# A macaron block on one core: query rows in two kinds, one scratch write per batch, four groups of position products per tile

## The reference

```
content = einsum('bhsp,bhtp->bhst', q + u, k)
pos     = relative_shift(einsum('bhsp,htp->bhst', q + v, sinusoid @ Wp + bp))
weights = softmax((content + pos) / sqrt(8));  out = (weights @ val) @ Wo + bo
```

## Time and profile before

| | us |
|---|---|
| median of the runs | 445.53 |
| the profiled execution: its time | 447.46 |
| its span, first to last instruction | 445.3 |
| VectorE busy | 398.2 (89%) |
| TensorE busy (matmuls) | 357.0 (80%) |
| ScalarE busy | 263.9 (59%) |
| GpSimd busy | 113.4 (25%) |

### The profile page before, as it was taken

The page is one execution under the profiler, slowest core; times in us unless marked ns, Lnnn a source line. Parts: engine busy times, 40 slices in busy tenths (PEclk is TensorE's granted clock), DMA queues, the critical chain, the costliest instruction groups (busy, mean ns, idle before and its releaser), DMA issues.

```text
span 445.3 us, 18049 instructions
## 1 busy us (share of the span) xinstructions
PE 357.0 (80%) x7328; PEld 288.1 (65%) x7328; DVE 398.2 (89%) x579; ACT 263.9 (59%) x650; POOL 113.4 (25%) x157
## 2 busy tenths in 40 slices
PE   1869898756979889898898987988989889676974
PEld 1647675645767767677676766776767767573664
DVE  8786988429999999999999999999999999948685
ACT  1666555316666666666666666666666666614980
POOL 7543745390020201202102022020120210025552
PEclk9988899969899999999999999999999999988898
DMA  7005147920322313213133132231321301500002
GB/s 213 1 1 186 51 148 245 296 62 12 81 57 43 81 26 87 68 31 84 40 65 75 19 88 56 44 80 20 88 64 30 89 7 25 75 18 2 0 26 71
DMA packets 60182, 30.67 MB, mean 69 GB/s; under 512 B 36880, under 2 KB 58928, under 8 KB 60016
## 3 DMA queue, kind: packets, MB, share of 16 engines
q1 hardware_dynamic: 59376, 29.22, 25.8%
q10 hardware_dynamic: 576, 0.73, 0.6%
q0 software_dynamic: 192, 0.18, 0.2%
HBM read 19.11 MB, written 11.01 MB: 68 GB/s over the span
## 4 chain that ended last, share of the span: by engine, by line
DVE 58%; issue 17%; PE 11%; ACT 5%; POOL 2%; SPq 2%; DMA 2%; DVEq 1%; POOLq 0%; ACTq 0%
DVE pT L894 30%; DVE negmax L886 19%; PE pair L1014 3%; ACT v_rep L602 2%; DVE xh L702 2%; ACT v_rep L590 1%; PE pair L969 1%; DVE v_rep L820 1%; DVE sqsum L814 1%; DMA qs_scratch<-pT 1%; SPq L309 1%; PE pair L1183 1%; DMA stage_k<-kc_scratch 1%; DVE stat L692 1%; PE pair L1116 1%
## 5 line engine op out<-in xcount | busy, mean ns | idle before, releaser
L633 ACT ACTIVATE probs<-pair,negmax 128x512 f32<-128x512 f32 x256 | 173.7, 683 | 111.3 <-DVE negmax L886 111.3
L886 DVE TENSOR_REDUCE negmax<-pair 128x2 f32<-128x1024 f32 x128 | 152.1, 1188 | 10.4 <-PE pair L1133 10.4
L894 DVE STREAM_TRANSPOSE pT<-probs 128x1024 f32<-128x1024 f32 x128 | 157.0, 1226 | 0.5 <-ACT probs L633 0.5
L1116 PE MATMUL pair<-stage_k,stage_c 128*32 128x512 f16 x1024 | 117.2, 408 | 47.4 <-ACT probs L633 40.8
L1122 PE MATMUL pair<-stage_z,stage_q 128*32 128x512 f16 x1024 | 111.4, 384 | 0.0
L1133 PE MATMUL pair<-stage_z,stage_q 128*32 128x438 f16 (+58 forms) x1024 | 102.9, 282 | 0.0
L508 POOL COPY v_diag<-v_rep 32x512 f32 (+1 forms) x64 | 38.9, 607 | 233.9 <-PE pair L1148 226.5
L1128 PE MATMUL pair<-stage_z,stage_q 128*32 128x16 f16 (+50 forms) x1024 | 97.9, 277 | 0.0
L1148 PE MATMUL pair<-pT,v_diag 128*32 128x128 f32 (+1 forms) x2176 | 93.3, 271 | 3.6 <-DVE pT L894 3.6
L1116 PEld LDWEIGHTS pair<-stage_k,stage_c 128*32 128x32 f16 x1024 | 50.7, 140 | 69.5 <-ACT probs L633 55.4
L1148 PEld LDWEIGHTS pair<-pT,v_diag 128*32 128x32 f32 x2176 | 73.3, 114 | 4.1 <-DVE pT L894 3.8
(11 more groups left out here) (112 smaller groups left out, 326.0 us busy)
## 6 DMA issues: line engine op xcount, KB each, us to landing
stage_z<-z_scratch SPq DMA_DIRECT2D x16, 254.0 KB
qs_scratch<-pT SPq DMA_DIRECT2D x12, 256.0 KB, 2.7
stage_q<-qs_scratch SPq DMA_DIRECT2D x126, 24.0 KB
stage_z<-z_scratch SPq DMA_DIRECT2D x16, 128.0 KB
qc_scratch<-pT SPq DMA_DIRECT2D x8, 256.0 KB, 3.5
kc_scratch<-pT SPq DMA_DIRECT2D x8, 256.0 KB, 3.5
stage_k<-kc_scratch SPq DMA_DIRECT2D x16, 128.0 KB
stage_z<-z_scratch SPq DMA_DIRECT2D x16, 127.5 KB
```

The lines of the kernel that those rows point to most:

```text
L633: nc.scalar.activation(probs[:, q % 6, :], score_pair(q // 2)[:, q % 2, :], ACT.Exp, bias=negmax[:, q % 8:q % 8 + 1], accum_out=rowsum[:, ...
L886: nc.vector.tensor_reduce(negmax[:, 2 * n % 8:2 * n % 8 + 2], score_pair(n)[:, :, :], AX.X, ALU.max, negate=True).then_inc(max_ready, 1)
L894: nc.vector.transpose(pT[:, par, 2 * n:2 * n + 2, :].rearrange("p a s -> p (a s)"), probs[:, 2 * n % 6:2 * n % 6 + 2, :].rearrange("p a s ...
L1116: mm(bank[32 * j:32 * j + 32, :], all_rows[:, 32 * j:32 * j + 32], stage_k[:, par, :], start=True, stop=False, skip_group_check=True)
```

## The change

The query scratch keeps, per batch and head element, the row of vl and the row of vh (576 columns each), written by one DMA. stage_q holds for each block of 64 query rows the rows themselves and the rows one group further on, side by side, and each row pair carries low and high halves. Positions come in two sets, high (low = 0) and low (low = 1), each a part of 512 columns and a part of ZR = 510 columns. So each tile has four groups of position products instead of three: for each set the left part and the right part. The low x low product, which was left out, is now part of the sum. The scratch of content queries and keys is laid out by head and batch. SP waits for GpSimd's copies before its first write of a batch, and writes in the order queries, content, keys.

```
-    qs_dram = nc.dram_tensor("qs_scratch", (D, 2, 3, B * S), F16, kind="Internal").ap()
-    qc_dram = nc.dram_tensor("qc_scratch", (D, 4, B * S), F16, kind="Internal").ap()
-    kc_dram = nc.dram_tensor("kc_scratch", (D, 4, B, S), F16, kind="Internal").ap()
-    z_dram = nc.dram_tensor("z_scratch", (D, 2, 3, 2 * S), F16, kind="Internal").ap()
+    qs_dram = nc.dram_tensor("qs_scratch", (D, 2, B, VW), F16, kind="Internal").ap()
+    qc_dram = nc.dram_tensor("qc_scratch", (H, B, 2, HP, 2, S), F16, kind="Internal").ap()
+    kc_dram = nc.dram_tensor("kc_scratch", (H, B, 2, HP, 2, S), F16, kind="Internal").ap()
+    z_dram = nc.dram_tensor("z_scratch", (D, 2, 4, 2 * S), F16, kind="Internal").ap()
...
-        stage_q = sb("stage_q", [128, 2, 3, B * S], F16)
+        stage_q = sb("stage_q", [128, 2, B * NI, 2, NG], F16)
-        stage_z = sb("stage_z", [128, 2, 3, ZW], F16)
+        stage_z = sb("stage_z", [128, 2, 2, S + ZR], F16)
...
         def stage_queries(eng, h, par, done, rows_i=range(NI)):
-            q_rows = qs_dram.rearrange("(h p) t k n -> h (p t) k n", p=HP)[h]
+            q_rows = qs_dram.rearrange("(h p) t b n -> h (p t) b n", p=HP)[h]
             for ii in rows_i:
                 i = NI - 1 - ii
-                src = q_rows.rearrange("r k (b m) -> r (k b) m", b=B)[:, :, i * NG:(i + 1) * NG]
-                dst = stage_q[16 * ii:16 * ii + 16, par, :, :].rearrange(
-                    "r k (b m) -> r (k b) m", b=B)[:, :, i * NG:(i + 1) * NG]
-                eng.dma_start(dst, src).then_inc(done, 16)
+                dst = stage_q[16 * ii:16 * ii + 16, par, :, :, :].rearrange("r (b i) k g -> r b i (k g)", b=B)[:, :, i]
+                eng.dma_start(dst, q_rows[:, :, i * NG:(i + 2) * NG]).then_inc(done, 16)
+
+        def write_queries(eng, b, r, done):
+
+            eng.dma_start(qs_dram[r, :, b, :], rep_ap(vl[r, b, :], [(VQ, 2), (1, VW)])).then_inc(done, 16)
+
+        def write_content(eng, b, h0, h1, done):
+            c = slice(b * S, (b + 1) * S)
+            for a in range(2):
+                eng.dma_start(qc_dram[h0:h1, b, a].rearrange("h p d n -> h (p d n)"), half[HP * h0:HP * h1, 0:2, c])\
+                    .then_inc(done, 16)
+
+        def write_keys(eng, b):
+            c = slice(b * S, (b + 1) * S)
+            for a in range(2):
+                eng.dma_start(kc_dram[:, b, a].rearrange("h p d n -> h (p d n)"),
+                              rep_ap(half[:, 2 + a, c], [(0, 2), (1, S)])).then_inc(k_out, 16)
...
-            for t, kind, src in ((0, 0, 0), (1, 0, 2), (0, 1, 0), (1, 1, 1), (0, 2, 2), (1, 2, 3)):
-                sp.dma_start(z_dram[:, t, kind, :], zs[:, src, :]).then_inc(z_out, 16)
+            for t in range(2):
+                sp.dma_start(z_dram[:, t, :, :], zs).then_inc(z_out, 16)
...
-                for kind, lo, hi in ((0, 0, ZW), (1, 0, S), (2, ZB0, ZW)):
-                    zr = z_rows[:, kind, :]
-                    src = bass.AP(zr.tensor, zr.offset + lo, [[1, NI]] + [list(zr.ap[0])] + [[1, hi - lo]])
-                    sp.dma_start(stage_z[:, par, kind, lo:hi], src).then_inc(staged[par], 16)
+                for low in range(2):
+                    for kind, lo, at, n in ((low, 0, 0, S), (2 + low, ZB0, S, ZR)):
+                        zr = z_rows[:, kind, :]
+                        src = bass.AP(zr.tensor, zr.offset + lo, [[1, NI]] + [list(zr.ap[0])] + [[1, n]])
+                        sp.dma_start(stage_z[:, par, low, at:at + n], src).then_inc(staged[par], 16)
...
-                sp.wait_ge(q_split, 2 * b + 1)
-                sp.dma_start(qs_dram[:, :, 1, c], rep_ap(vh[:, b, :], [(0, 2), (1, S)])).then_inc(q_out, 16)
                 sp.wait_ge(v_extended, 2 * b + 2)
-                sp.dma_start(qs_dram[:, :, 0, c], rep_ap(vl[:, b, :], [(NG, 2), (1, S)])).then_inc(q_out, 16)
-                sp.dma_start(qs_dram[:, :, 2, c], rep_ap(vh[:, b, NG:], [(0, 2), (1, S)])).then_inc(q_out, 16)
-
+                write_queries(sp, b, slice(0, D), q_out)
                 sp.wait_ge(q_split, 2 * b + 2)
...
-            for par, n in ((0, 0), (0, 1), (0, 2), (1, 0), (1, 1)):
-                nc.vector.memset(stage_q[:, par, n, :].bitcast(U32), 0).then_inc(stage_zero, 1)
+            for par in range(2):
+                for b in (0, 2):
+                    nc.vector.memset(stage_q[:, par, b * NI:(b + 2) * NI, :, :].bitcast(U32), 0)\
+                        .then_inc(stage_zero, 1)
...
-            nc.gpsimd.memset(stage_q[:, 1, 2, :].bitcast(U32), 0).then_inc(stage_zero, 1)
...
+                for low in range(2):
+                    for j in range(4):
+                        a0 = 128 * j + NI * q
+                        n = a0 + NI
+                        m0 = S - NI - a0
+                        mm(bank[32 * j:32 * j + 32, 0:n], stage_q[:, par, :, 0, j * NQ + q],
+                           stage_z[:, par, low, m0:m0 + n], start=False, stop=False, skip_group_check=True)
+                    for j in range(4):
+                        a0 = 128 * j + NI * q
+                        n = S - a0 - 2
+                        ins = mm(bank[32 * j:32 * j + 32, a0 + 2:S], stage_q[:, par, :, 1, j * NQ + q],
+                                 stage_z[:, par, low, S:S + n], start=False, stop=low == 1, skip_group_check=True)
```

More of the change, by code:

```diff
@@ L53 @@
 LOADS_FIRST = 6
[L54 removed]
+LOADS = 17
+ZR = ZW - ZB0
 def macaron_kernel(nc, ins, out):
     x_d, w12_d, vectors_d, rows_d, wqkv_d, wo_d, wp_emb_d, ident_d = ins
[L61 to L64 removed]
+    qs_dram = nc.dram_tensor("qs_scratch", (D, 2, B, VW), F16, kind="Internal").ap()
+    qc_dram = nc.dram_tensor("qc_scratch", (H, B, 2, HP, 2, S), F16, kind="Internal").ap()
+    kc_dram = nc.dram_tensor("kc_scratch", (H, B, 2, HP, 2, S), F16, kind="Internal").ap()
+    z_dram = nc.dram_tensor("z_scratch", (D, 2, 4, 2 * S), F16, kind="Internal").ap()
     at_dram = nc.dram_tensor("attn_scratch", (H, HP, 16, 128), F32, kind="Internal").ap()
@@ L119, in macaron_kernel @@
         uh, ul, kh, kl = (half[:, n, :] for n in range(4))
+        VQ = 2 * (14336 - 8192)
         vl = pTf[:, 8192:8192 + B * VW // 2].bitcast(F16).rearrange("p (b n) -> p b n", b=B)
@@ L291, in stage_content @@
         def stage_content(eng, h, par, b, done):
-            c_rows = qc_dram.rearrange("(h p) t n -> h (p t) n", p=HP)[h]
+            rows32 = qc_dram.rearrange("h b a p d n -> h b (a p d) n")[h][b]
             dst = stage_c[32 * b:32 * b + 32, par, :].rearrange("r (j b m) -> r j b m", j=4, b=B)[:, :, b]
-            src = c_rows[:, b * S:(b + 1) * S].rearrange("r (j m) -> r j m", j=4)
-            eng.dma_start(dst, src).then_inc(done, 16)
+            eng.dma_start(dst, rows32.rearrange("r (j m) -> r j m", j=4)).then_inc(done, 16)
@@ L298, in stage_keys @@
         def stage_keys(eng, h, par, done):
-            k_rows = kc_dram.rearrange("(h p) t b n -> h b (p t) n", p=HP)[h]
-            eng.dma_start(stage_k[:, par, :], k_rows).then_inc(done, 16)
+            eng.dma_start(stage_k[:, par, :], kc_dram.rearrange("h b a p d n -> h (b a p d) n")[h]).then_inc(done, 16)
         def stage_queries(eng, h, par, done, rows_i=range(NI)):
-            q_rows = qs_dram.rearrange("(h p) t k n -> h (p t) k n", p=HP)[h]
+            q_rows = qs_dram.rearrange("(h p) t b n -> h (p t) b n", p=HP)[h]
@@ L340, in _ @@
             for b in range(B):
-                c = slice(b * S, (b + 1) * S)
-                sp.wait_ge(q_split, 2 * b + 1)
-                sp.dma_start(qs_dram[:, :, 1, c], rep_ap(vh[:, b, :], [(0, 2), (1, S)])).then_inc(q_out, 16)
                 sp.wait_ge(v_extended, 2 * b + 2)
-                sp.dma_start(qs_dram[:, :, 0, c], rep_ap(vl[:, b, :], [(NG, 2), (1, S)])).then_inc(q_out, 16)
-                sp.dma_start(qs_dram[:, :, 2, c], rep_ap(vh[:, b, NG:], [(0, 2), (1, S)])).then_inc(q_out, 16)
+                write_queries(sp, b, slice(0, D), q_out)
                 sp.wait_ge(q_split, 2 * b + 2)
-                for t, src in ((0, uh), (2, ul)):
-                    sp.dma_start(qc_dram[:, t:t + 2, c], rep_ap(src[:, c], [(0, 2), (1, S)]))\
-                        .then_inc(u_out[b], 16)
+                write_content(sp, b, 0, H, u_out[b])
                 if b < B - 1:
@@ L356, in _ @@
                     sp.wait_ge(k_split_last, 1)
[L357 to L361, removed]
+                write_keys(sp, b)
+            sp.wait_ge(q_out, 16 * B)
+            sp.wait_ge(stage_zero, 6)
             stage_queries(sp, 0, 0, staged[0], range(NI - 2))
@@ L495, in _ @@
             ffn(0)
-            pool.wait_ge(q_out, 16 * 3 * B)
-            pool.wait_ge(stage_zero, 8)
+            pool.wait_ge(q_out, 16 * B)
+            pool.wait_ge(stage_zero, 6)
             stage_queries(pool, 0, 0, staged_first, range(NI - 2, NI))
@@ L880, in _ @@
             dve.wait_ge(k_out, 32 * B)
-            dve.wait_ge(q_out, 16 * 3 * B)
+            dve.wait_ge(q_out, 16 * B)
             def row_max(h, n):
@@ L1107, in scores @@
```

(2 more changed lines are left out.)

3 lines of the change are left out of this document (1 added, 2 removed).

## The result

The changed kernel takes 458.41 us (median of four, 457.95 to 460.17) against 445.43 us (four, 445.25 to 446.58): ratio 1.0279, 95% interval 1.025 to 1.0307. It is slower, by 13 us; the forecast was 437.8. The profiled execution has a span of 458.1 us, against 445.3.

The account below looks back on a forecast made before the run. VectorE, busy all 18.06 us of a head, was taken as the bound, with gains only before head 0 and at the start: 4.9 + 2.1 + 0.7 = 7.7 us, from 445.53 to 437.8 us; range 435 to 443.5.

Parts of the forecast that it names:

- rival B: TensorE's loop over heads outgrows its instruction buffer; five returns fetch, 0.8 us each, 4 in all: 442 us; chance 0.2.
- Staging: Passage from projections to attention: earlier last query write and cheaper query loads land head 0's keys sooner; gain 4.9 us.
- Clock: TensorE before head 0: shorter idling keeps its clock full for the first tiles; gain 2.1 us, 0 if it falls.
- Memsets: Start of the kernel: smaller stage_q means fewer memsets, so the first LayerNorm statistics start earlier; gain 0.7 us.
- Score matmuls: Inside heads: a ragged pair costs what one full group costs, hidden in TensorE's 2.5 us idle per head; cost 0.
- Rival C: Inside heads: added ragged groups cost 0.21 us each, so TensorE becomes the bound; 452 us; chance 0.05.
- Rival D: Start of head 0: another wait, such as GpSimd's staging, holds it until about 93 us; 445 us; chance 0.04.
- rival A: Before head 0: query loads and last write stay slow and the clock falls, half the gain; 441.5 to 442.5; chance 0.15.
- the forecast's case: Whole kernel: gain of 6 to 9.5 us, giving 436 to 439.5 us; chance 0.56.

Follow-up runs that it names:

- without the loop: TensorE's heads 3 to 14 written out instead of looped: the kernel before then took 446.67 us (ratio 0.9986), the changed kernel 442.01 us (0.9865).
- with 16 products: Kernel before with each full-width low x high product of 512 columns issued as two of 256, loop kept: 463.95 us, ratio 1.0372.
- with 12 products: Changed kernel with the right-hand product of the low positions left out, loop kept: 442.87 us, ratio 0.9885.
- shifted: Changed kernel, loop kept, with 50 tiny filler matmuls (100 instructions) before head 0 to move the loop: 459.84 us, ratio 1.0234.
- written-out version: Changed kernel with TensorE's heads 3 to 14 written out instead of a loop: 442.01 us, ratio 0.9865 against the kernel before.
- with fillers: Changed kernel, heads written out, plus 16 unused fp32 matmuls of 128 columns in TensorE's wait before head 0: 440.99 us, ratio 0.986.
- the repeat: Changed kernel with heads written out, no fillers, timed again beside its filler counterpart: 442.37 us, ratio 0.9889 against the kernel before.

## Why the prediction was wrong, step by step

**The step that failed: rival B, with a chance of 0.2 and 0.8 us per return.** It is what happens, and a return costs 3.3 us. Two things went wrong in it. First its chance. The rows said that the body of before spans seven pieces and that one more is fetched ahead: eight pieces held. The new body was put at "eight or nine" pieces, and still got a chance of 0.2. The Trainium skill ("Runtime: NRT & Kernel Launch", Instruction fetch mechanics) gives TensorE room for 2,048 instructions, eight pieces, and I compared this with the matmuls and weight loads of the body, 1,792, not with its pieces and the one ahead. Held against pieces the same figure agrees with all runs: seven and one ahead stay (no fetch, 0.2 us per return), eight and one ahead don't (nine fetches per pass, over 4 us). That the piece fetched ahead is what pushes out the first one fits all of this, but is not shown: the runs only show the limit between seven and eight. The same section's rule that a taken branch out of a two-page window forces a fetch does not hold here: the loop of seven pieces jumps back over six without any.

Second its price. The cover was read rightly: 1.93 us plus 0.7. The return itself was bounded by one late fetch of 1.12 us in straight code, but a fetch behind a branch is another thing: at the first return 1.3 us until it begins, 1.4 for itself, 1.3 until the branch ends. Some 1.8 us of it are left uncovered there, inside the bound of 2.1, but over twice the 0.8 that was taken. What the bound did not hold is the clock, 1.0 us at that return, which falls behind this stop (at four of the five returns of after), and that later branches take up to 5.1 us. The forecast looked at the clock before head 0 and did not ask what a new stop elsewhere would do to it. A slip besides: the high end of the range, 1.2 us per return on the forecast's 437.8, is 443.8 and not 443.5.

In the sum of the forecast the returns stood at 0. For the profiled execution it gives 439.8 us, and that took 460.17: of the 20.4 us between them 16.7 are the returns, 2.5 the tail, and 1.2 what the way to the end of head 0 gained less than forecast (6.5 instead of 7.7).

**Staging, forecast 4.9 us.** SP's queue in after (columns as in the earlier trace rows):

```profile
76.32 0.62 SPq L311 DMA_DIRECT2D qs_scratch<-pT  x1
...
76.98 1.30 SPq L316 DMA_DIRECT2D qc_scratch<-pT  x2
...
78.33 2.25 SPq L322 DMA_DIRECT2D kc_scratch<-pT  x2
80.70 4.67 SPq L307 DMA_DIRECT2D stage_q<-qs_scratch  x6
85.41 0.59 SPq L300 DMA_DIRECT2D stage_k<-kc_scratch  x1
```

The last query write went out earlier than forecast (76.32, where 78.6 less 0.7 for the start was expected) and the loads began at 80.70. But they cost 0.78 us each on average (one took 1.28), not 0.47: their form, with 16 rows, was not like line 296 with its 32. The key load went out at 85.41 (84.1 expected) and landed in 2.26 us instead of 3.66 (the chain of waits of after, columns as in the earlier trace rows):

```profile
85.41 2.26 DMA stage_k<-kc_scratch
```

So the first score came at 87.81, where 87.9 follows from the forecast. The loads' error was cancelled by the other two, which is luck. Compared with before, 93.64 became 87.81, 5.8 us, 0.6 of it from the start, in this pair of traces. In other executions the first score came at 92.0 and 92.8 with the staging of before (without the loop, and with 16 products) and at 88.5 to 88.8 with the new one (without the loop, twice, with 12 products, and shifted). By these the staging is worth some 4 us rather than 5.

**Clock, forecast 2.1 us.** The first pair took 2.07 us instead of 2.97, and the second wait rose to 1.30 from 0.93: worth 0.5 us. In the written-out version (first trace) it was worth nothing: the clock fell, and TensorE had idled 3.89 us. The size of the term was about right for a clock that stays (1.87 and 0.16 us with fillers, where 1.65 and 0.1 were forecast); the claim that it stays was wrong. The forecast counted 1.6 us of idling from the last work of before, at 87.06. In after that work ends at 84.61, so the start of head 0 came earlier and the idling was still 3.20 us.

**Memsets, forecast 0.7 us.** The first statistics ran at 5.59 instead of 6.14, the first normalization at 8.17 instead of 8.76: 0.6 us. Right.

**Score matmuls, forecast 0 on the path.** Right, but a ragged pair is not quite free: 0.62 us more per head, 39 ns a tile, where 25 were allowed for and 160 would decide. Rival C is out. Rival D is out, since head 0 starts behind the key load, and earlier than before. As for rival A, the written-out version earns 4.9 us by the medians of its own chip (446.89 to 442.01) and 5.5 by the repeat (447.84 to 442.37), not 7.7: about the forecast less the clock. Taken from 445.5 that would be 440.0 to 440.6, between the forecast's case (436 to 439.5) and A (441.5 to 442.5).

## What to carry to other kernels

Before adding instructions to an engine's loop, count its body in pieces of 256 from the program's start, with the ragged ends and one more that is fetched ahead: on TensorE a loop over seven pieces returned in 0.2 us, one over eight took 4.0 to 5.7 us at every return, and 100 instructions more or less ahead of the loop decided it here. The fetches per pass on the instruction queue, none or nine, tell which of the two it is. Written-out code cost nothing here (0.9986 [0.9964, 1.0008]), so the change is worth having without its loop (442 us, 1.1 to 1.4% faster than before). And where a change adds a stop to TensorE, price the tiles behind it at half clock too: behind the stops of 3.5 to 4.5 us at the returns of after the clock fell at four of five, worth 1.0 us at the first.

## What was not expected of the hardware

- A branch on TensorE's sequencer took 0.2 us in one kernel and 4.2 to 4.6 us in another that differs in the place of the loop alone; the two are 25 us apart (447.42 and 472.54).
- The row of waits named ScalarE as the releaser of TensorE at a return, with 3.5 us; the sequencer's own rows named the branch.
- TensorE's clock fell to 0.50 behind waits of 3.2 and 3.5 us, when the engine had begun to work again (88.00 to 90.00, and 181.00 to 182.00); in the kernel before it fell within the wait, some 4 us in, and in the changed kernel with 50 fillers 1.7 us after its last work. A long stop is not needed: with 12 products it also fell twice in the loop (145.4 and 200.0 us) behind stops of 1.1 and 0.8 us, and two heads took 0.3 us longer. Work of no use in the wait before head 0 made the kernel before 0.4% faster.
- Six loads of 16 rows with pieces of 256 B took SP 4.67 us to issue, 0.78 each on average; four loads of 32 rows with such pieces took 1.89 in the kernel before.
